# A composed-weight product whose moving table is half empty: its two low-order products folded into one, over a copy made by ScalarE

## What is computed

```python
def _layer(x, style, w, b, mw, mb, typ):
    s = style @ mw.T + mb
    weight = SCALE * w * s[:, None, :, None]
    demod = lax.rsqrt(jnp.sum(weight * weight, axis=(2, 3)) + EPS)
    weight = weight * demod[:, :, None, None]
    ...
x = x + _L0_attn_ref(_L0_cond_ref(x, cond_512, ...), ...)
x = x + _L0_ffn_ref(_L0_cond2_ref(x, cond_512, ...), ...)
```

## Time and profile before

| | |
|---|---|
| median of 3 runs | 1338.85 us (1338.64 to 1340.85) |
| the profiled execution | 1337.98 us, its span 1336.1 us |
| busy: PE, PEld | 1293.9 us (97%), 1226.3 us (92%) |
| busy: DVE, ACT, POOL | 1044.7 us (78%), 798.9 us (60%), 806.3 us (60%) |
| chain that ended last | PE 86%, DVE 5%, POOL 4%, ACT 2% |
| mean granted TensorE clock | 0.995 of full speed |

### The profile page before, as it was taken

One profiled execution on the slowest core, in us unless ns is written; L12 is line 12 of the kernel. 1 busy time (PEld: TensorE's weight loads), 2 busy tenths in 40 slices (PEclk: granted clock), 3 DMA queues, 4 the chain that ended last, 5 costly groups with the idle time before them and its releaser, 6 DMA issues.

```text
span 1336.1 us, 22883 instructions
## 1 busy us (share of the span) xinstructions
PE 1293.9 (97%) x8127; PEld 1226.3 (92%) x8127; DVE 1044.7 (78%) x2442; ACT 798.9 (60%) x1625; POOL 806.3 (60%) x611
## 2 busy tenths in 40 slices
PE   3789999999999999999999999999999999999998
PEld 3589899899899999899999999999999999999998
DVE  7878878778877778778778888787878878787873
ACT  4587787778777787775445544545554554545440
POOL 6468887666676677664555545555555555555542
PEclk9899999999999999999999999999999999999999
DMA  3234444444455654452542523425243342524322
GB/s 129 77 105 134 133 133 133 133 132 133 132 140 148 155 150 141 126 160 79 119 117 85 147 77 103 130 77 151 81 123 109 95 136 78 151 80 120 111 84 88
DMA packets 86274, 158.20 MB, mean 118 GB/s; under 512 B 26633, under 2 KB 48402, under 8 KB 86034
## 3 DMA queue, kind: packets, MB, share of 16 engines
q1 hardware_dynamic: 84898, 154.79, 41.5%
q10 hardware_dynamic: 1264, 1.96, 0.5%
HBM read 93.79 MB, written 33.56 MB: 95 GB/s over the span
## 4 chain that ended last, share of the span: by engine, by line
PE 86%; DVE 5%; POOL 4%; ACT 2%; issue 1%; DMA 1%; SPq 0%; DVEq 0%; POOLq 0%; ACTq 0%
PE psum L1770 28%; PE psum L1772 27%; PE psum L1771 27%; PE psum L1884 2%; POOL xs_l L931 1%; DVE psum L1544 1%; DMA w3T<-in_w_dram 1%; POOL vs_l L926 0%; POOL vbuf L910 0%; POOL vbuf L906 0%; PE psum L283 0%; DVE y_l L1490 0%; POOL vbuf L908 0%; DVE a_l L1520 0%; DVE a_f L1525 0%
## 5 line engine op out<-in xcount | busy, mean ns | idle before, releaser
L1770 PE MATMUL psum<-wt_h,u_h 128*128 128x386 f32 (+1 forms) x760 | 260.9, 343 | 0.0
L1772 PE MATMUL psum<-wt_h,u_l 128*128 128x386 f32 (+1 forms) x760 | 257.9, 339 | 0.0
L1771 PE MATMUL psum<-wt_l,u_h 128*128 128x386 f32 (+1 forms) x760 | 257.6, 339 | 0.0
L1544 DVE STREAM_TRANSPOSE psum<-vbuf 32x256 f32<-32x256 f32 x480 | 218.8, 456 | 11.8 <-ACT vbuf L1137 0.7
L1520 DVE SCALAR_TENSOR_TENSOR a_l<-psum,tabs,a_h 128x512 fp32r<-128x512 f32 x128 | 95.9, 751 | 158.7 <-ACT a_h L1119 158.6
L906 POOL TENSOR_TENSOR vbuf<-vbuf 128x512 f32<-128x512 f32 x64 | 97.1, 1518 | 190.7 <-ACT vbuf L1151 190.7
L920 POOL TENSOR_TENSOR vm_f<-vm_f 128x512 f32<-128x512 f32 x64 | 82.7, 1292 | 177.5 <-DVE vm_l L1514 177.1
L1144 ACT ACTIVATE vbuf<-psum,tabs 128x512 f32<-128x512 f32 x128 | 105.2, 822 | 117.4 <-PE psum L1772 113.5
L1770 PE MATMUL psum<-a_h,vm_h 128*128 128x256 f32 x512 | 148.2, 289 | 3.2 <-ACT vbuf L1144 3.0
L1771 PE MATMUL psum<-a_l,vm_h 128*128 128x256 f32 x512 | 145.7, 285 | 0.0
L1770 PEld LDWEIGHTS psum<-wt_h,u_h 128*128 128x128 f32 x760 | 143.5, 189 | 2.2
(11 more groups left out here) (309 smaller groups left out, 3803.7 us busy)
## 6 DMA issues: line engine op xcount, KB each, us to landing
vm_f<-vv SPq DMA_DIRECT2D x256, 112.0 KB, 4.5
xin<-in_x_ph_dram SPq DMA_DIRECT2D x32, 512.0 KB, 5.0
xr<-in_x_row_dram SPq DMA_DIRECT2D x32, 512.0 KB, 4.2
x1d<-xr SPq DMA_DIRECT2D x64, 256.0 KB, 3.3
xin<-x1d SPq DMA_DIRECT2D x32, 512.0 KB, 5.4
xr<-x1d SPq DMA_DIRECT2D x64, 256.0 KB, 5.9
xo<-in_b_base_dram SPq DMA_DIRECT2D x32, 512.0 KB, 5.9
out_dram<-xo SPq DMA_DIRECT2D x31, 512.0 KB, 2.9
```

Source lines behind the costliest of these rows:

```text
L1544: ins = V.transpose(ps_x[to, :, :].rearrange("p b (k n) -> p b k n", n=P)[:, :, :, frm], v3[frm, :, :].rearrange("p b (k n) -> p b k n", n ...
L1770: nc.tensor.matmul(to, stat_h, mov_h, start=first_ and n == 0, stop=False, skip_group_check=True)
L1771: nc.tensor.matmul(to, stat_h, mov_l, start=False, stop=False, skip_group_check=True)
L1772: ins = nc.tensor.matmul(to, stat_l, mov_h, start=False, stop=end, skip_group_check=True)
```

## The change

Block 2 of `step2` uses only the lower 64 partitions of its stationary operand: high x high and low x high are two products that each use half of it. The change puts the two into one: the high part of the fifth tap is copied into the upper 64 partitions of `c1_l`'s block 2, beside its low part in the lower 64, and the product runs over a new table `rt_h` that has the fifth tap's part of `r_h` in both halves. Block 2 then has two products, `c1_h` x `r_l` and (`c1_l` with the copy) x `rt_h`, and `step2` eight.

What comes with it: on ScalarE one copy for each tile, `fifth(g)`, which waits for VectorE's `c1_lo`, placed in the turn behind `turned(i - 1)` (or, with `by_blocks`, ahead of the wait for the transposes), and in `first_turns` behind `composed1(0)` and `composed2(0)`; two more copies in each of the two `r_high`; on TensorE a wait for `rt_hi` at tiles 0 and 32 and one for `c1_fifth` ahead of the last product. For memory, `hw` moves onto `em1` and `zero` onto `vv`, for which the first `composed_out` waits until the transfer of `zero` is done.

```diff
+        sh.rt_h = sb("rt_h", [P, 2, TAPS, C], FR)
...
-    hw = sb("hw", [P, ER])
...
+    hw = sh.em1[:, 0, 0, :]
+
+    zero = vv[0:1, 0:PAD // C, :].rearrange("p k c -> p (k c)")
...
-        zero = tb("zero", [1, PAD])
...
-                sp.dma_start(sh.kpad[0:1, 0:PAD], zero[:, :]).then_inc(k_out, 16)
+                sp.dma_start(sh.kpad[0:1, 0:PAD], zero).then_inc(k_out, 16)
...
-            G.memset(zero[:, :], 0.0).then_inc(zero_set, 1)
+            G.memset(zero, 0.0).then_inc(zero_set, 1)
...
@@ r_high (ScalarE)
                 A(r_h[:, c, :, :], r_f[:, c, :, :], ACT.Copy).then_inc(r_hi, 1)
+                for half in HALF:
+                    ins = A(rt_h[half, c, :, :], r_f[LOW, c, :, :], ACT.Copy)
+                ins.then_inc(rt_hi, 1)
...
+            def fifth(g):
+
+                act.wait_ge(c1_lo, at(g))
+                A(c1_l[HIGH, 2, :, :], c1_h[LOW, 2, :, :].bitcast(F32), ACT.Copy).then_inc(c1_fifth, 1)
+
@@ first_turns (ScalarE)
                 composed1(0)
+                fifth(0)
                 edge_lay_first(nc, act, sh)
...
                 composed2(0)
+                fifth(1)
                 inputs(1)
@@ body (ScalarE)
                     pair_sums(i)
                 if by_blocks(i - 1):
+                    if here(i + 1):
+                        fifth(i + 1)
 
                     act.wait_ge(tr_done, at(i - 1))
...
                     if here(i - 1):
                         turned(i - 1)
+                    if here(i + 1):
+                        fifth(i + 1)
                     if turn_is(i, 1):
                         toeplitz()
...
@@ composed_out (VectorE)
                 ve.wait_ge(step2_done, at(g))
+                if g == 0:
+
+                    ve.wait_ge(k_out, 16)
@@ step2 (TensorE)
                 if g in (0, TILES):
                     pe.wait_ge(r_lo, c + 1)
+                    pe.wait_ge(rt_hi, c + 1)
                 pe.wait_ge(c1_lo, at(g))
-                for n in range(3):
-                    ins = product(ps_step[:, C * n:C * (n + TAPS)],
-                                  [(c1_h[:, n, :, :].rearrange("p b o -> p (b o)"), c1_l[:, n, :, :].rearrange("p b o -> p (b o)"),
-                                    r_h[:, c, :, :].rearrange("p d o -> p (d o)"), r_l[:, c, :, :].rearrange("p d o -> p (d o)"))],
-                                  n == 0, n == 2)
-                ins.then_inc(step2_done, 1)
+                for n in range(2):
+                    product(ps_step[:, C * n:C * (n + TAPS)],
+                            [(c1_h[:, n, :, :].rearrange("p b o -> p (b o)"), c1_l[:, n, :, :].rearrange("p b o -> p (b o)"),
+                              r_h[:, c, :, :].rearrange("p d o -> p (d o)"), r_l[:, c, :, :].rearrange("p d o -> p (d o)"))],
+                            n == 0, False)
+
+                nc.tensor.matmul(ps_step[:, C * 2:C * (2 + TAPS)], c1_h[:, 2, :, :].rearrange("p b o -> p (b o)"),
+                                 r_l[:, c, :, :].rearrange("p d o -> p (d o)"), start=False, stop=False, skip_group_check=True)
+                pe.wait_ge(c1_fifth, at(g))
+                nc.tensor.matmul(ps_step[:, C * 2:C * (2 + TAPS)], c1_l[:, 2, :, :].rearrange("p b o -> p (b o)"),
+                                 rt_h[:, c, :, :].rearrange("p d o -> p (d o)"), start=False, stop=True, skip_group_check=True)\
+                    .then_inc(step2_done, 1)
```

More of the change, by code:

```diff
@@ L407, in program @@
     tabs, iota8, vec = sh.tabs, sh.iota8, sh.vec
-    r_h, r_l, x1w = sh.r_h, sh.r_l, sh.x1w
+    r_h, r_l, rt_h, x1w = sh.r_h, sh.r_l, sh.rt_h, sh.x1w
     bt_h, bt_l, toep_h, toep_l = sh.bt_h, sh.bt_l, sh.toep_h, sh.toep_l
@@ L527, in program @@
     style_in, style1_in, wT_in, wT1_in = sem("style_in"), sem("style1_in"), sem("wT_in"), sem("wT1_in")
-    r_terms, r_sum, r_hi, r_lo = sem("r_terms"), sem("r_sum"), sem("r_hi"), sem("r_lo")
+    r_terms, r_sum, r_hi, r_lo, rt_hi, c1_fifth = (sem("r_terms"), sem("r_sum"), sem("r_hi"), sem("r_lo"),
+                                                    sem("rt_hi"), sem("c1_fifth"))
     w3_in, cm_in, cm1_in, m0_in = sem("w3_in"), sem("cm_in"), sem("cm1_in"), sem("m0_in")
```

## The result

The changed kernel takes **1343.53 us** (median of 8 runs, 1341.72 to 1345.66) against 1339.25 for the kernel before, run beside it: a ratio of 1.0033, 95% interval 1.0022 to 1.0044. It is slower by 4.3 us, where 1337.4 was forecast with a range up to 1340.5. The profiled execution took 1343.22 us, with a span of 1341.3.

A forecast was written before the change was run, and what follows sets the result against it. A chain of other engines bounds the first 91 us, TensorE's queue the rest. Steady gain 4.1 us (2.8 + 2.3 - 0.3 - 0.7) less 2.7 for the start gave 1.4 gained: median 1337.4 us, range 1333.5 to 1340.5.

The forecast's parts named there:

- The step that failed: First network: the copy fits between `turned` and the evacuation without delaying it, hidden by 0.03 us.
- 19 x 0.147 = 2.8 us: First network: 19 turns each keep the removed product's full 0.147 us, 2.8 us gained.
- The rival with this sign: First network: the copy pushes the evacuation every turn, 19 turns lose 0.06 us each; 1341.4 us, chance 0.10.
- The start: Before the steady turns: fifth(1) waits on ScalarE and delays what stands behind it, 2.7 us lost.
- The chain that was named: Start: fifth(1) delays inputs(1), then POOL's `xs_l`, which with `as_l` holds up VectorE's `vm_l` and `fs`; 2.7 us lost.
- TensorE is granted its lower level (1.2 GHz) more often: Rival, start: longer TensorE gaps bring four more clock dips, 6.8 us; 1344.3 us, chance 0.07.
- The two copies of `r_high(0)`, put at 0: Start: they move `y_h` and the first `xs_h` by 0.72 us; effect taken as 0 (-0.5 to +0.7).
- `r_high(1)`: Turn 6, first network: two added copies delay an already late evacuation, 0.7 us lost (0 to 0.9).
- The second network: Evacuation limits the gain to 0.08 us a turn; 28 turns give 2.3 us, the copy being free.
- Turns released by GpSimd: First network: in 11 turns `third` waits for POOL's `vs_l`, so the 0.147 us gain is lost again.
- its margin of 0.03 us: First network: slack between the copy's end, 302.70, and the evacuation's own wait for its product, until 302.73.
- the rival of a pushed evacuation: First network: the copy delays the evacuation every turn, 0.06 us lost in each of 19; 1341.4 us, chance 0.10.

The follow-up runs named there:

- e1: Changed kernel with fifth(1) moved behind inputs_high(1) on ScalarE in the start; 1340.5 us, 1.0010 of the kernel before.
- e3: Changed kernel whose copy reads and writes the upper 64 partitions, leaving out high x high of the fifth tap; 1342.45 us, one run.
- e5: Changed kernel with the copy kept and step2's nine products restored; 1346.6 us, 1.0055 of the kernel before.
- e6: Changed kernel with the two added rt_h copies moved out of each r_high to later places on ScalarE; 1343.47 us, 1.0034 of the kernel before.
- e2: Changed kernel whose copy reads and writes the lower 64 partitions, leaving out low x high of the fifth tap; 1337.76 us, 0.9993 of before.
- e4: Changed kernel without the copy from the third tile on, leaving out high x high of the fifth tap; 1337.46 us, 0.9988 of before.
- e9: Changed kernel with the copy of tiles 2 to 34 on VectorE, written with one PSUM operand; 1338.29 us, 0.9993 of the kernel before.
- e10: Changed kernel with the edits of e9, e1 and e6 together; 1335.7 us, 0.9974 of the kernel before.
- e7: Changed kernel with the copy of tiles 2 to 34 on VectorE, from SBUF to SBUF; 1348.5 us, 1.0074 of the kernel before.
- e11: Changed kernel with the first network's copy behind the evacuation on ScalarE, eighth product inside pair's second half; 1340.87 us, 1.0011 of before.

## Why the prediction was wrong

- **The step that failed** is the copy's in the first network: "an instruction behind it can begin 0.1 us before its end", from which it was "hidden, by 0.03 us". The 0.1 us is true of neighbours that write from the same start partition, as in the earlier trace rows. The copy writes the upper half; it begins 0.02 us after its neighbour's end, and the next one 0.03 after its own, so it takes 0.36 us from `u_h`'s end to the evacuation where 0.10 were reckoned. Instead of 19 x 0.147 = 2.8 us gained, a usual turn loses 0.05 to 0.1, and the 28 turns with no other event lose 1.24 us in all, since those that GpSimd releases lose nothing. The turn at 324 us, where ScalarE was a little late before too (T+0.37), loses 0.40; it loses 0.35 to 0.39 in e1, e3, e5 and e6, 0.08 in e2 and nothing in e4, e9 and e10, so this is the copy too. The rival with this sign took 0.06 a turn and came out at 1341.4.
- **The start** came out near, 2.7 us forecast and 3.05 measured, partly by luck. The chain that was named is there, but it makes 2.18 us of it (`fs` at 50.03, forecast at 50.6): VectorE did get through between `xs_l` and `as_l`, with one of its two `vm_l`. The forecast had POOL keep the ports, from the earlier trace rows at 20.56; the same rows show the other case at 21.8, where the first `y_l` ends at 21.97, right behind `m_l` (21.82) and inside `xs_l`. The other 0.87 us goes with the lower clock, which stood among the rivals ("TensorE is granted its lower level (1.2 GHz) more often"): one more dip of some 3 us, not four. The two copies of `r_high(0)`, put at 0, let `y_l` through 1.5 us sooner, and `fs` in e1 begins 0.58 sooner than before.
- **`r_high(1)`**: 0.7 us (0 to 0.9) forecast, 1.86 measured. The two copies take 0.96 us from 174.23 to 175.19, where 0.72 were taken from the earlier trace rows. In the other kernels with the tables in this place, e7 aside (e1, e2, e3, e4, e5, e9, e11) the turn loses 0.80, 0.52, 0.77, 0.73, 1.06, 1.01 and 0.69 us; with them moved (e6, e10), 0.02 and -0.03. So the term itself was about right. In the changed kernel's profile ScalarE is besides at `c_h` 0.8 us later against T than before (173.26 - 174.16 against 169.43 - 171.12), ahead of those copies, and this is the transfer of `vm_f`: ScalarE waited 1.42 us for it, where it waited 0.63 before and not at all in e1.
- **Turns not in the sum.** The turns at 308 and 499 us lose 0.61 and 0.55. In that at 308 ScalarE waits for the same transfer, which it did not before:

```profile
301.92 1.40 ACT L1099 ACTIVATE vm_h<-vm_f 128x512 fp32r<-128x512 f32 x2 [1.02 <-DMA vm_f<-vv]
```

  Ahead of that at 499 it waits 0.86 us for it, 0.56 before. e9 and e10 lose 0.47 to 0.66 in both of them too, e4 and e5 only in the second, so that neither the copy nor the eight products are needed for it. Why the transfer is late is open.
- **The second network** was right in its mechanism: 0.08 us a turn forecast, 0.07 measured (23.41 to 23.34), which makes 2.0 over 28 turns. That all of it comes to 2.4 against 2.3 is in part luck. Four turns (at 614, 638, 662 and 924 us of the kernel before) took 23.61 to 23.80 us and take 23.33 or 23.34 now; in e5, with its nine products, three of them take 23.40 or 23.41, so that what had lengthened them, 1.1 us in all, did not hang on the product. Others, the most that at 854 us with 0.47, became longer than usual and take part of it back. What lengthens such turns was not traced.
- **Turns released by GpSimd** were right: those at 187 and 203 us stay within 0.03.
- **The sum** therefore reads +3.05 for the start, +1.86 for the turn of `r_high(1)`, +1.56 for the turns at 308, 324 and 499 us, +1.24 for the rest of the first network, -2.40 for the second: +5.3, the span's 5.2. The usual turns put 4.0 us between forecast and result (2.8 gained against 1.24 lost).

The forecast called its margin of 0.03 us thin and gave the rival of a pushed evacuation 0.10. Its evidence for the overlap was one pair of neighbours that both write all partitions, and two small copies into the same half. The trace of before held the case that was needed 1.3 us further on in the timeline of ACT, where these copies pass from the lower half to the upper:

```profile
16.37 0.49 ACT L1018 ACTIVATE xr<-w 64x128 f32<-64x128 f32 x2
16.87 0.31 ACT L1018 ACTIVATE em<-w 64x128 f32<-64x128 f32 x1
17.09 0.29 ACT L1018 ACTIVATE xr<-w 64x128 f32<-64x128 f32 x1
```

The first of the upper half begins at 16.87, 0.01 us behind the end of the last of the lower (16.37 + 0.49), and takes 0.31 us, as the new copy does; the next, into the same half, begins 0.09 before that one's end. So it is the change of half that costs, not the upper half as such. Back to the lower half, at 17.59 us, it costs again: that copy begins 0.01 behind its neighbour's end and takes 0.31.

## What to carry to other kernels

A product taken off TensorE is worth its distance only up to the evacuation that it covered: look for the second-latest release before the sum, and put nothing on the engine that delivers it. Where a helper copy must go somewhere, price it by its gaps on both sides, in the place where it will stand and with the partitions it will write, and by what it shares ports with. And an early wait in a hand-written order costs all that is queued behind it, on two further engines here.

## What the runs showed of the hardware

- ScalarE's instructions overlap by about 0.1 us when they write from the same start partition. A copy to the upper 64 partitions began 0.02 to 0.03 us behind the end of its neighbour, and the neighbour behind it 0.02 to 0.03 after its own end; to the lower half it began 0.12 before (changed kernel, e2, e3).
- On VectorE the form of a copy decided: 64x128 from SBUF to SBUF took 0.25 to 0.32 us four times of 33, and 0.92 to 3.58 otherwise, and always ended 0.08 to 0.09 us behind a POOL operation that it had met (e7); with one operand in PSUM all 33 took 0.28 (e9, e10).
- Between two GpSimd instructions in a row VectorE mostly got through, but not always: the first `vm_l` of the changed kernel did, between `xs_l` and `as_l`, and so did 30 of e7's 33 copies; three of them, and e10's first `y_l` (5.27 us long, from 18.97), stood through more than one. What decides it was not found.
- Starts of nearly the same work had a granted clock of 0.84 to 0.95 from the second tile's `step2` to the third's, and with it a first T up to 1.85 us apart (changed kernel, e2, e3, e4, e5, e11).
